# A normalised 3x3 convolution on TensorE: the first two images alone, each as two halves on all 128 partitions, before the first pair

## The reference

```
g = v.reshape(B, 32, 2, H, W)
m = mean(g, axis=(2, 3, 4)); s = var(g, axis=(2, 3, 4))
gn = ((g - m) / sqrt(s + 1e-5)).reshape(v.shape)
out = x + conv3x3(gn, sign(W), padding=1)
```

## Time and profile before

| | |
|---|---|
| median of 3 runs | 202.28 us (201.34, 202.35, 202.28) |
| span of the profiled execution | 200.7 us |
| TensorE, busy in matmuls | 191.2 us, 95% |
| GpSimd busy | 166.7 us, 83% |
| VectorE busy | 165.3 us, 82% |
| ScalarE busy | 149.7 us, 75% |
| HBM read and written | 257 GB/s over the span |

### The profile page before, as it was taken

The page is one execution under the profiler, slowest core; times in us unless marked ns, Lnnn a source line. Parts: engine busy times, 40 slices in busy tenths (PEclk is TensorE's granted clock), DMA queues, the critical chain, the costliest instruction groups (busy, mean ns, idle before and its releaser), DMA issues.

```text
span 200.7 us, 10042 instructions
## 1 busy us (share of the span) xinstructions
PE 191.2 (95%) x4482; PEld 168.4 (84%) x4482; DVE 165.3 (82%) x363; ACT 149.7 (75%) x142; POOL 166.7 (83%) x85
## 2 busy tenths in 40 slices
PE   1999999999999999999999999999999999999990
PEld 0478888879858988988999988899998999889990
DVE  2799999996999997799988779998779999627392
ACT  3185999799989289899909989972998999595000
POOL 1029786999999999999999997999999899999500
PEclk9999999999999999999999999999999999999999
DMA  6978977871787988868697887868887883906274
GB/s 216 362 217 292 331 246 252 289 209 44 306 243 291 297 316 282 282 248 278 242 301 296 275 327 276 325 228 321 326 241 296 266 319 152 381 13 238 116 283 175
DMA packets 18698, 52.17 MB, mean 260 GB/s; under 512 B 2080, under 2 KB 5024, under 8 KB 18656
## 3 DMA queue, kind: packets, MB, share of 16 engines
q1 hardware_dynamic: 18656, 51.54, 72.9%
HBM read 25.84 MB, written 25.69 MB: 257 GB/s over the span
## 4 chain that ended last, share of the span: by engine, by line
PE 65%; ACT 14%; DVE 13%; DMA 3%; issue 1%; SPq 0%; DVEq 0%; ACTq 0%
PE psum L738 65%; ACT halves L424 5%; DVE stats L500 5%; ACT xnorm L418 4%; DMA xbuf<-in_x_dram 3%; ACT moved L437 3%; DVE xbuf L570 2%; DVE xbuf L556 1%; DVE xbuf L580 1%; DVE own L508 1%; ACT line_halves L447 1%; ACT std L413 1%; DVE xbuf L544 1%; ACT lines_norm L451 1%; DVE halves L538 1%
## 5 line engine op out<-in xcount | busy, mean ns | idle before, releaser
L738 PE MATMUL psum<-halves,w_taps 64*64 64x385 f16 (+8 forms) x4140 | 183.4, 325 | 0.5 <-DVE halves L532 0.4
L738 PEld LDWEIGHTS psum<-halves,w_taps 64*64 64x64 f16 x4140 | 156.7, 107 | 19.3 <-ACT moved L437 0.9
L330 POOL TENSOR_TENSOR halves<-xnorm,halves 128x784 f16<-128x784 f32 (+5 forms) x35 | 91.6, 2637 | 20.0 <-ACT xnorm L418 19.7
L500 DVE BATCH_NORM_STATS2 stats<-xbuf 128x6 f32<-128x448 f32 x112 | 60.8, 613 | 4.3 <-DMA xbuf<-in_x_dram 4.1
L424 ACT ACTIVATE halves<-xbuf,coef 128x784 f16<-128x784 f32 (+5 forms) x35 | 50.7, 1449 | 3.0 <-DVE coef L525 2.8
L418 ACT ACTIVATE xnorm<-xbuf,coef 128x784 f32<-128x784 f32 (+5 forms) x35 | 50.5, 1443 | 0.0
L437 ACT ACTIVATE moved<-psum 64x784 f32<-64x784 f32 (+1 forms) x30 | 25.5, 850 | 7.9 <-PE psum L738 7.3
L345 POOL TENSOR_TENSOR xbuf<-xbuf,moved 128x784 f32<-128x784 f32 (+1 forms) x15 | 29.3, 1956 | 0.4 <-ACT moved L437 0.4
L570 DVE SCALAR_TENSOR_TENSOR xbuf<-psum,xbuf 64x784 f32<-64x784 f32 (+1 forms) x32 | 28.2, 881 | 1.0
L556 DVE SCALAR_TENSOR_TENSOR xbuf<-psum,xbuf 128x784 f32<-128x784 f32 x21 | 20.3, 967 | 7.6 <-PE psum L738 7.4
L371 POOL TENSOR_TENSOR line_halves<-lines_norm,line_halves 128x1512 f16<-128x1512 f32 (+1 forms) x10 | 20.9, 2120 | 0.5 <-ACT lines_norm L451 0.5
(11 more groups left out here) (36 smaller groups left out, 72.0 us busy)
## 6 DMA issues: line engine op xcount, KB each, us to landing
xbuf<-in_x_dram SPq DMA_DIRECT2D x48, 448.0 KB, 4.6
out_dram<-xbuf SPq DMA_DIRECT2D x43, 392.0 KB, 4.0
xbuf<-in_x_dram SPq DMA_DIRECT2D x16, 224.0 KB, 4.1
out_dram<-xbuf SPq DMA_DIRECT2D x5, 504.0 KB, 3.9
out_dram<-xbuf SPq DMA_DIRECT2D x5, 448.0 KB, 3.8
out_dram<-xbuf SPq DMA_DIRECT2D x5, 364.0 KB, 4.1
out_dram<-xbuf SPq DMA_DIRECT2D x5, 252.0 KB, 4.1
out_dram<-xbuf SPq DMA_DIRECT2D x1, 224.0 KB, 3.8
```

Of the source, the lines that this page charges most:

```text
L330: nc.gpsimd.tensor_tensor(at(halves[:, k % HRING, 1, :], a, b), at(xnorm[:, k % NRING, :], a, b), at(halves[:, k % HRING, 0, :], a, b), AL ...
L500: nc.vector.bn_stats(stats[:, n, :], xbuf[:, s, n * STAT:(n + 1) * STAT]).then_inc(blocks_ready, 1)
L738: mm = pe.matmul(outs[:, :, left:right], weights, ins[:, :, left + dx:right + dx], start=first_step, stop=last_step)
```

## The change

Images 0 and 1 become items of their own (SINGLES = 2), and the pairs follow as items 2 to 16, so that pair k of before is item k+1, and the set WINOGRAD holds the same images as before. A single image lies on all 128 partitions: its upper 28 rows on LOW with one row of the lower half behind them, its lower 28 rows on HIGH with one row of the upper half ahead of them. Missing outer rows are zeroed by GpSimd. It has one home unit and one away unit of two blocks, and chunks of 16 and 14 rows. Statistics are taken in 4 pieces of 392 pixels, copied from each half of the partitions to the other, and then aggregated over both.

Image 0 is loaded by SyncE and ScalarE, two 64-partition DMAs each, and the raw weights by ScalarE instead of SyncE. TensorE's warm-up waits for no load any more; WARM_UP goes from 17 to 12 rounds and KEEP_WARM from 4 to 10. VectorE makes the upper half of the first chunk of items 0, 1 and 2 (early_upper); normalise and lo of these chunks are with ScalarE and GpSimd. The away unit of each single image is moved by ScalarE and added by GpSimd. weights_of_products comes after item 2.

```
-WARM_UP = 17
-KEEP_WARM = 4
+WARM_UP = 12
+KEEP_WARM = 10
+SINGLES = 2
+EARLY = 3
-WINOGRAD = (3, 6, 9, 12, 14)
+WINOGRAD = (4, 7, 10, 13, 15)
...
     def home_units(k):
+        if k < SINGLES:
+            return [[(1, 7), (15, 7)]]
...
     def away_units(k):
+        if k < SINGLES:
+            return [[(8, 7), (22, 7)]]
...
     def by_scalar(k, i):
-        return k != LAST and i == (0 if k in WINOGRAD else 1)
+        return k != LAST and i == (0 if k in WINOGRAD or k < SINGLES else 1)
...
     def chunks(k):
-        if k < 2:
+        if k < SINGLES:
+            return [(0, 16), (16, 30)]
+        if k == SINGLES:
             return [(0, 15), (15, 29), (29, 43), (43, 56)]
...
+        SPLIT_LOADS = [(LOW, 0, 14, 1), (HIGH, HALF - 1, HALF + 14, 0), (LOW, 14, HALF + 1, 15), (HIGH, HALF + 14, H, 15)]
+
         def start_load(eng, k, n):
+            if k < SINGLES:
+                lanes, a, b, to = SPLIT_LOADS[n]
+                eng.dma_start(at(xbuf[lanes, k, :], to, to + b - a), at(one(x, k), a, b)).then_inc(loaded[k][n], 16)
+                return
...
         @block.sync
-            for n in range(NPIECE):
+            for n in (0, 2):
                 start_load(sp, 0, n)
-            sp.dma_start(w_raw[:], w.rearrange("o c h w -> o (c h w)")).then_inc(w_loaded, 16)
             for n in range(NPIECE):
                 start_load(sp, 1, n)
...
+            def store_image(k):
+                sp.wait_ge(home_done, home_before(k) + 1)
+                wait_away(k, 0)
+                for n, (lanes, first, frm) in enumerate(((LOW, 0, 1), (HIGH, HALF, 1), (LOW, 14, 15), (HIGH, HALF + 14, 15))):
+                    sp.wait_ge(*ended[-3])
+                    sp.dma_start(at(one(out, k), first, first + 14),
+                                 at(xbuf[lanes, k, :], frm, frm + 14)).then_inc(stored[k][n], 16)
+                    ended.append((stored[k][n], landed(k)))
...
-                if k >= 1:
+                if 1 <= k <= SINGLES:
+                    store_image(k - 1)
+                if k > SINGLES:
                     store_unit(k - 1, 1)
-                store_unit(k, 0)
+                if k >= SINGLES:
+                    store_unit(k, 0)
...
         @block.gpsimd
+            for k in range(SINGLES):
+                nc.gpsimd.memset(at(xbuf[LOW, k, :], 0, 1), 0.0).then_inc(edges_ready, 1)
+                nc.gpsimd.memset(at(xbuf[HIGH, k, :], HALF + 1, HALF + 2), 0.0).then_inc(edges_ready, 1)
...
-                if k >= 2 and k - 2 not in WINOGRAD and k != WINOGRAD[0]:
+                if k >= 2 and k - 2 not in WINOGRAD and k not in (SINGLES, WINOGRAD[0]):
+                    add_away(k - 2, 0 if k - 2 < SINGLES else 1)
+                for c in range(len(chunks(k))):
+                    lo(k, c)
+                    if (k, c) == (SINGLES, 1):
+                        add_away(k - 2, 0)
+                if k == WINOGRAD[0]:
                     add_away(k - 2, 1)
...
-                if k == 0:
+                if k == SINGLES:
                     weights_of_products()
...
         @block.scalar
+            for n in (1, 3):
+                start_load(act, 0, n)
+            act.dma_start(w_raw[:], w.rearrange("o c h w -> o (c h w)")).then_inc(w_loaded, 16)
...
                 if k >= 2 and k - 2 not in WINOGRAD:
-                    move_away(k - 2, 1)
+                    move_away(k - 2, 0 if k - 2 < SINGLES else 1)
...
                 for c in range(len(chunks(k))):
-                    if (k, c) != (0, 0):
+                    if not by_vector(k, c):
                         hi(k, c)
-                        normalise(k, c)
+                    normalise(k, c)
...
+            def split_stats(k):
+                for n in range(NSPLIT):
+                    if n % 2 == 0:
+                        dve.wait_ge(loaded[k][n], landed(k))
+                        dve.wait_ge(loaded[k][n + 1], landed(k))
+                    nc.vector.bn_stats(stats[:, n, :], at(xbuf[:, k, :], 1 + 7 * n, 8 + 7 * n)).then_inc(blocks_ready, 1)
+                dve.wait_ge(blocks_ready, stats_before(k + 1))
+                for here, there in ((LOW, HIGH), (HIGH, LOW)):
+                    nc.vector.tensor_copy(stats[here, NSPLIT:2 * NSPLIT, :], stats[there, 0:NSPLIT, :]).then_inc(crossed, 1)
...
-            def early_chunk():
...
+            def early_upper(k):
+                a, b = chunks(k)[0]
+                dve.wait_ge(coef_ready, 3 * k + 2)
+                nc.vector.tensor_scalar(at(halves[:, k, 0, :], a, b), at(xbuf[:, k, :], a, b),
+                                        coef[:, k, 0:1], coef[:, k, 1:2], ALU.mult, ALU.add).then_inc(hi_early, 1)
...
-            for k in range(2):
-                pair_stats(k, range(NSTAT))
+            dve.wait_ge(edges_ready, 2 * SINGLES)
+            for k in range(SINGLES):
+                split_stats(k)
                 aggregate(k)
                 scale(k)
-                if k == 0:
-                    early_chunk()
-            for k in range(NP):
+                early_upper(k)
+            pair_stats(2, range(NSTAT))
+            aggregate(2)
+            add_home(0, 0)
+            scale(2)
+            early_upper(2)
+            pair_stats(3, range(NSTAT))
+            add_home(1, 0)
+            aggregate(3)
+            for k in range(SINGLES, NP):
...
-            pe.wait_ge(loaded[0][0], 16)
             pe.wait_ge(filler_ready, 1)
             warm(WARM_UP)
...
-                if k == 0:
+                if k < EARLY:
                     for half in range(2):
                         for here, there in zip(home[:2], away[:2]):
```

More of the change, by code:

```diff
@@ L36 @@
 class Block:
-    pair: int
+    item: int
     unit: int
@@ L63, in conv_preact_kernel @@
     NSTAT = HW // STAT
-    NP = B // 2
+    HALF = H // 2
+    SPLIT_STAT = 7 * W
+    NSPLIT = HALF * W // SPLIT_STAT
+    NP = SINGLES + (B - SINGLES) // 2
     LAST = NP - 1
@@ L143, in chunks_by, with by_vector, uppers_by, stats_before @@
     def chunks_by(k, c):
-        return chunks_before(k) + c
+        return chunks_before(k) + c + 1
+    def by_vector(k, c):
+        return k < EARLY and c == 0
+    def uppers_by(k, c):
+        return chunks_by(k, c) - min(k + 1, EARLY)
+    def stats_before(k):
+        return NSPLIT * min(k, SINGLES) + NSTAT * max(k - SINGLES, 0)
     PIECES = [(0, 16), (16, 32), (32, 48), (48, 56)]
@@ L192, in conv_preact_kernel @@
         blocks_ready = sem("blocks_ready")
+        edges_ready = sem("edges_ready")
+        crossed = sem("crossed")
         coef_step = sem("coef_step")
@@ L220, in both, with one @@
         def both(t, k):
-            return t[2 * k:2 * k + 2].rearrange("b c h w -> (b c) (h w)")
+            first = SINGLES + 2 * (k - SINGLES)
+            return t[first:first + 2].rearrange("b c h w -> (b c) (h w)")
+        def one(t, k):
+            return t[k].rearrange("c h w -> c (h w)")
         block = ctx.enter_context(nc.Block())
@@ L342, in add_away @@
                 else:
-                    away = at(slot, 28 * i, 28 * i + 28).rearrange("p (n m) -> p n m", m=2 * BN)[:, :, BN:]
+                    top = 28 * i + (1 if k < SINGLES else 0)
+                    away = at(slot, top, top + 28).rearrange("p (n m) -> p n m", m=2 * BN)[:, :, BN:]
                     part = moved[:, m % 2, 0:2 * BN].rearrange("p (n m) -> p n m", m=BN)
@@ L680, in last_chunk @@
             def last_chunk(b):
-                k = b.pair
+                k = b.item
                 return next(n for n, (a, z) in enumerate(chunks(k)) if min(b.first + b.rows, H - 1) < z)
             def wait_upper(b):
-                k = b.pair
+                k = b.item
                 if b.product is None:
-                    if (k, last_chunk(b)) == (0, 0):
-                        pe.wait_ge(hi_early, 1)
+                    if by_vector(k, last_chunk(b)):
+                        pe.wait_ge(hi_early, k + 1)
                     else:
-                        pe.wait_ge(hi_ready, chunks_by(k, last_chunk(b)))
+                        pe.wait_ge(hi_ready, uppers_by(k, last_chunk(b)))
                 else:
@@ L695, in wait_lower @@
             def wait_lower(b):
-                k = b.pair
+                k = b.item
                 if b.product is not None:
                     pe.wait_ge(line_lo_ready, 2 * winograd_before(k) + (2 if b.product == 1 else 1))
-                elif (k, last_chunk(b)) == (0, 0):
-                    pe.wait_ge(lo_early, 1)
                 else:
@@ L720, in step @@
                         dy, dx = t // KW - 1, t % KW - 1
-                        r0, r1 = max(b.first, -dy), min(b.first + b.rows, H - dy)
+                        if b.item < SINGLES:
+                            top, end = (1, HALF + 2) if lanes == LOW else (0, HALF + 1)
+                        else:
+                            top, end = 0, H
+                        r0, r1 = max(b.first, top - dy), min(b.first + b.rows, end - dy)
```

(2 more changed lines are left out.)

54 lines of the change are left out of this document (21 added, 33 removed).

## The result

The change made the kernel slower. In the first comparison the changed kernel took 207.96 us and the kernel before 201.63 us (medians of 5 runs each, their profiled executions included), ratio 1.028, 95% interval 1.025 to 1.031. The prediction was 203.6 us with a range of 201.4 to 205.3. Its direction was right and its size was not.

The account below looks back on a forecast made before the run. TensorE, 95% busy, was taken as released at 59.05 us by the other engines' queues. Earlier start worth 0, GpSimd 2.2 us later less 0.9 slack gives +1.3: 202.28 + 1.3 = 203.6 us, range 201.4 to 205.3.

Parts of the forecast that it names:

- What TensorE's start is worth: First convolution at 11.0 us, 1.35 earlier than before; worth 0 because later waits cover it.
- The cold convolution of the rival: Items 0 and 1 begin at 1.2 GHz after TensorE idles; item 0 takes 6 us more, 207 us; chance 0.04.
- The step that decides: GpSimd's queue from item 2 to item 5: lo of item 3 at 35.2 us, 2.2 later; +1.3 us after slack.
- the 0.9 of slack in the prediction's sum: TensorE's spare time before it needs GpSimd's lo of item 5, subtracted from GpSimd's 2.2 us delay.
- The step that failed: VectorE's queue ahead of GpSimd's: statistics of image 0 end at 6.5 us, coefficients of item 2 come at 21.7.
- the end of image 0's statistics: VectorE's first statistics, after the first loads: end at 6.5 us, bounds 6.1 and 8.8.
- the copies of statistics: VectorE's two copies across the partition halves: 0.4 us, bounds 0.15 and 0.6.
- SyncE's cost: Two images stored by 8 DMAs instead of 4: cost taken as zero, without cover beyond that.
- The slow-loads rival: Half-partition loads are slow: statistics at 7.9 to 8.8 us instead of 6.5, time 205 to 205.9; chance 0.14.
- The cold rival: Convolution of items 0 and 1 begins at 1.2 GHz, 6 us more with 1.4 covered, 207 us; chance 0.04.
- Slower: Outcome above 203.3 us: chance 0.48, against 0.38 for same and 0.14 for faster.

Follow-up runs that it names:

- e_load_pair: Changed kernel with items 0 and 1 loaded by four 128-partition transfers each, taking other pixels: 206.65 against 202.47 us for the kernel before, ratio 1.023.
- e_warm: Changed kernel with WARM_UP 26 instead of 12 rounds: median 208.63 against 202.47 us for the kernel before, ratio 1.029.
- e_cross: Changed kernel with both copies of statistics across the partition halves made by ScalarE instead of VectorE: 207.56 against 202.47 us for the kernel before.
- e_weights: Changed kernel with weights_of_products put back after item 1 in GpSimd's queue: 207.07 against 202.29 us for the kernel before, ratio 1.024.
- e_cross1_weights: Changed kernel, own loads, item 1's statistics copied by ScalarE and weights_of_products after item 1: 206.37 against 201.71 us for the kernel before, ratio 1.022.
- e_pair_cross1_weights: Changed kernel with e_load_pair's loads, item 1's statistics copied by ScalarE, weights_of_products after item 1: 204.46 against 202.29 us for the kernel before, ratio 1.011.
- e_after: The changed kernel itself, measured again beside the kernel before: 207.65 against 202.47 us, ratio 1.028.
- b_split: Kernel before with each load piece of pairs 0 and 1 issued as two 64-partition transfers from one queue: 203.97 against 201.71 us, ratio 1.010.
- e_load: Changed kernel, items 0 and 1 loaded by 128-partition transfers with the right pixels, source half by half: 229.3 to 232.4 us against 202.29 for the kernel before.

## Why the prediction was wrong

**What TensorE's start is worth: right, though the start itself was not.** It came at 13.3 us instead of 11.0: the raw weights landed at 8.4 us instead of 6.4 (at 6.9 with e_load_pair's loads, so 1.5 of it goes with the slow transfers), and the ten rounds ran at the lower level. That cost nothing, since the start was covered: e_warm began 1.6 us earlier for nothing. The cold convolution of the rival did not happen; the ten rounds in front of it took the lower level's price.

**The step that decides: right, with ScalarE's queue close behind.** GpSimd's queue from item 2 to item 5 took 8.63 + 23.33 us, predicted 8.8 and the same as before. Across the kernels the end follows the start of that queue's lo of item 5 (pair 4 before) nearly one to one, in the profiled executions in which no late load holds TensorE. The last column goes to the start of VectorE's last instruction, since what comes behind it, the last store above all, varies (2.7 us in e_warm, 3.9 to 4.8 in the others):

| kernel | lo of item 3 | lo of item 5 | span | span less lo of item 5 | last VectorE instruction less lo of item 5 |
|---|---|---|---|---|---|
| before | 33.00 | 56.33 | 200.7 | 144.4 | 196.68 - 56.33 = 140.4 |
| e_load_pair | 37.27 | 60.59 | 204.3 | 143.7 | 200.20 - 60.59 = 139.6 |
| e_cross | 38.24 | 61.57 | 205.1 | 143.5 | 201.19 - 61.57 = 139.6 |
| e_warm | 38.86 | 62.19 | 204.5 | 142.3 | 201.82 - 62.19 = 139.6 |
| e_weights | 37.49 | 60.82 | 205.2 | 144.4 | 200.44 - 60.82 = 139.6 |
| e_cross1_weights | 36.23 | 59.56 | 203.5 | 143.9 | 199.40 - 59.56 = 139.8 |
| e_pair_cross1_weights | 34.78 | 58.11 | 202.0 | 143.9 | 197.74 - 58.11 = 139.6 |

The kernel before stands 0.7 to 0.8 above the others because lo was there before TensorE needed it: that is the 0.9 of slack in the prediction's sum. The table alone does not show that GpSimd decides and not ScalarE: in the three kernels with weights_of_products moved GpSimd waits 0.4 us for ScalarE ahead of lo of item 3, and both queues start from VectorE's coefficients of item 2.

**The step that failed: two terms in VectorE's queue ahead of it were mis-sized.** The path was the one of the sum. First, the end of image 0's statistics: 6.5 us was taken, with 6.1 and 8.8 as bounds, and 8.5 measured. The prediction had the row that told it (248 GB/s where the 64-partition weights were due) and set it aside "since halves of both sides are in flight together". They were, from two queues, and it did not help: 250 GB/s in e_after, 255 in b_split from one queue, 358 in e_load_pair. This is 2.0 us. The upper bound of 8.8 held; but the stated range ended at 205.3, below the 205.9 that the prediction itself gave for that bound. Second, the copies of statistics: 0.4 us was taken for each item, with 0.6 as upper bound. Item 0's took 0.38, item 1's 2.24, since they wait for GpSimd (0.38 for item 1 too in e_load, with GpSimd idle). The bound came from rows where the operation runs alone; no row of before showed a VectorE copy beside GpSimd. This is 1.85 us. Together 3.85, which put GpSimd at 38.8 instead of 35.2 us and TensorE at 65.5 instead of 61.85. Predicted were 1.3 us in the end; with 3.6 more it is 4.9, and 5.2 to 6.3 were measured.

**What stays open.** The rest, 0.3 to 1.4 us, has no cause shown. Late loads are a candidate: the prediction took SyncE's cost as zero without cover, and in the two profiled executions of the changed kernel VectorE waits for loads and TensorE for VectorE after 100 us (TensorE 4.7 us in the first, 1.5 in e_after's; none in the kernel before). But those are the two longest runs, and of the others there is no trace. That SyncE's additional DMAs cause it was not tried. How the two delays add was not measured cleanly either, since the versions that move the copies to ScalarE bring waits of ScalarE's queue with them; e_load_pair gained 2.25 us at the statistics, gave 0.7 of it back in longer copies, and arrived 1.55 earlier at GpSimd. None of the versions beats the kernel before.

**The chances.** The slow-loads rival (205 to 205.9, 0.14) had the right cause for half of the miss, and it had no room for the copies. The cold rival's 207 (0.04) is nearer as a number, by luck, since its mechanism did not occur. Slower had 0.48, the largest of the three.

## What to carry to other kernels

When an engine is 95% busy, look for the point from which it runs without a break, and ask what released it there: an earlier start ahead of that point is worth only what the other queues gain as well. Splitting a tile to use all partitions earlier can cost more in its transfers than it saves in bytes: half the bytes at 250 instead of 390 GB/s was here a gain of 1 us at the statistics, paid for with a longer chain behind. And a row in the profile that gives a price for the new form is worth more than an argument why this case will be different.

## What the runs showed of the hardware

- With the first loads going to 64 partitions each, 246 to 255 GB/s flowed from 2.5 to 6.5 us, with 128-partition ones 334 to 395, at a DMA share of 0.97 to 1.06 in both (all profiles but e_load's; b_split against the kernel before has the same bytes and queue, 255 and 388). Such transfers to opposite halves, in flight from two queues, are no faster (e_after, 250) than from one (b_split, 255). The Trainium skill ("SBUF — State Buffer", "Can I just issue two DMAs to hit both halves?") answers that question with no, since only one transfer over all 128 partitions reaches all ports; the runs agree.
- A transfer whose source has an outermost dimension of 2 used 2 of 16 DMA engines: share 0.13 and 52 GB/s (e_load, one execution).
- A VectorE copy of 24 values on 64 partitions takes 0.17 us alone and up to 1.6 us beside GpSimd: each ended within 0.04 us of the end of a GpSimd subtraction (e_after), and two took 0.38 us with GpSimd idle (e_load).
- Statistics and float32 adds from psum kept their durations beside GpSimd's subtractions: three statistics take 1.69 us without GpSimd and seven 3.71 beside it (before, at 7.77 and 14.07), an add of 128x784 0.96 us without (e_after, at 23.57) and 0.97 beside it (at 33.28).
- From 2.5 to 6.5 us the profile's granted clock reads 1.00, though the rounds of the warm-up stand 0.37 us apart, which is 1.2 GHz for their four matmuls of 448 columns (e_after).
